# Where the inputs of the experts of rows 5 to 7 are scaled: ScalarE in four pieces, or GpSimd in two steps

## The reference, cut to what matters

```
h = h + attention(layernorm(h))
x = layernorm(h)                                   # over the 64 channels
mu, var = mean(x), var(x)
xn = (x - mu) * rsqrt(var + EPS) * gamma + beta    # 64 channels
logits = xn @ Wr + br;  w = softmax of the top 2 of 8
for e in range(8):
    hid = gelu(xn @ W1[e] + b1[e])                 # 128 wide
    y += (hid @ W2[e] + b2[e]) * w[e]
h = h + y
```

## Time and profile before

| what | value |
|---|---|
| device time, median of 3 runs | 415.62 us (415.4 to 415.87) |
| the profiled execution's own time | 415.76 us |
| its span, first to last instruction | 413.9 us |
| busy TensorE, weight loads | 389.1 us (94%), 313.9 us (76%) |
| busy VectorE, ScalarE, GpSimd | 350.8 us (85%), 324.6 us (78%), 260.3 us (63%) |
| granted TensorE clock | 1.0 over the whole span |
| the loop over the units | from about 315 us to the end |

### The profile page before, as it was taken

One profiled execution on the slowest core, in us unless ns is written; L12 is line 12 of the kernel. 1 busy time (PEld: TensorE's weight loads), 2 busy tenths in 40 slices (PEclk: granted clock), 3 DMA queues, 4 the chain that ended last, 5 costly groups with the idle time before them and its releaser, 6 DMA issues.

```text
span 413.9 us, 6363 instructions
## 1 busy us (share of the span) xinstructions
PE 389.1 (94%) x1988; PEld 313.9 (76%) x1988; DVE 350.8 (85%) x850; ACT 324.6 (78%) x555; POOL 260.3 (63%) x389
## 2 busy tenths in 40 slices
PE   5798879999999999999999998999997999998996
PEld 2586568888888888888888887877875877785773
DVE  4887689888988888898888979999987899889885
ACT  1263588999999988898887765578787999996993
POOL 0575787787778779877788466586521765343552
PEclk9999999999999999999999999999999999999999
DMA  6900010222132222212222000000000000000001
GB/s 205 357 3 0 2 25 27 53 52 47 31 51 52 34 46 52 51 34 44 52 50 52 1 1 2 1 2 1 2 2 1 1 2 13 15 13 13 14 13 26
DMA packets 15849, 14.94 MB, mean 36 GB/s; under 512 B 9796, under 2 KB 10568, under 8 KB 15560
## 3 DMA queue, kind: packets, MB, share of 16 engines
q1 hardware_dynamic: 15816, 14.54, 14.4%
HBM read 13.42 MB, written 1.11 MB: 35 GB/s over the span
## 4 chain that ended last, share of the span: by engine, by line
PE 70%; DVE 17%; ACT 5%; issue 5%; POOL 1%; DMA 1%; SPq 1%; POOLq 0%; DVEq 0%; ACTq 0%
PE ps L1497 62%; PE ps L1520 5%; DVE hid L1379 2%; ACT w_all L869 1%; DVE stats L999 1%; PE ps L1528 1%; ACT x L863 1%; DVE x L1379 1%; DVE hh L1280 1%; DVE kstat L1220 1%; DVE x L1236 1%; PE ps L1703 1%; DMA xn<-in_w_f 1%; DVE qmax L1232 1%; DVE qsum L1246 1%
## 5 line engine op out<-in xcount | busy, mean ns | idle before, releaser
L704 ACT ACTIVATE hid<-ps,b_fold 128x512 f32<-128x512 f32 x128 | 84.0, 681 | 21.3 <-PE ps L1497 20.9
L1073 DVE TENSOR_TENSOR hid_lo<-hid,hid_hi 128x1024 fp32r<-128x1024 f32 x64 | 78.7, 1229 | 25.4 <-ACT hid_hi L709 25.1
L1497 PE MATMUL ps<-xn_hi,w_all 128*128 128x512 f32 x256 | 87.4, 402 | 0.6 <-DVE xn_lo L1068 0.6
L1497 PE MATMUL ps<-hid_hi,w_all 128*128 128x512 f32 x256 | 85.0, 393 | 0.0
L709 ACT ACTIVATE hid_hi<-hid 128x1024 fp32r<-128x1024 f32 x64 | 67.9, 1061 | 2.0
L1497 PEld LDWEIGHTS ps<-xn_hi,w_all 128*128 128x128 f32 x256 | 48.4, 189 | 10.8 <-issue 0.9
L1497 PEld LDWEIGHTS ps<-hid_hi,w_all 128*128 128x128 f32 x256 | 48.1, 188 | 9.9
L1497 PE MATMUL ps<-xn_lo,w_all 128*128 128x512 f32 x128 | 49.9, 390 | 0.0
L1497 PE MATMUL ps<-hid_lo,w_all 128*128 128x512 f32 x128 | 49.8, 389 | 0.0
L1497 PE MATMUL ps<-hid_hi,ew 128*128 128x512 f32 x131 | 41.4, 402 | 0.7 <-ACT memT L807 0.4
L999 DVE BATCH_NORM_STATS2 stats<-ps 128x6 f32<-128x128 f32 x160 | 35.2, 281 | 2.8 <-PE ps L1520 2.8
(11 more groups left out here) (231 smaller groups left out, 913.0 us busy)
## 6 DMA issues: line engine op xcount, KB each, us to landing
rstd_row<-roots SPq DMA_DIRECT2D x29, 256.0 KB, 3.7
hh<-in_tokens SPq DMA_DIRECT2D x8, 256.0 KB, 7.9
hid<-in_w SPq DMA_DIRECT2D x1, 1024.0 KB, 7.2
rstd_row<-in_w SPq DMA_DIRECT2D x1, 1024.0 KB, 10.2
out<-hh SPq DMA_DIRECT2D x7, 128.0 KB, 2.0
ew_raw<-in_expert_w SPq DMA_DIRECT2D x1, 512.0 KB, 9.8
roots<-rstd SPq DMA_DIRECT2D x29, 2.0 KB, 1.4
ew_raw<-in_expert_w SPq DMA_DIRECT2D x1, 256.0 KB, 9.9
```

The source lines that it names most:

```text
L704: act.activation(hid[:, j % 2, f, :], bank[f], ACT.Gelu, bias=b1_fold[:, j // B * F + f:j // B * F + f + 1]).then_inc(gelu_done, 1)
L1073: dve.tensor_tensor(hid_lo[:, j % 2, 2 * p:2 * p + 2, :], hid[:, j % 2, 2 * p:2 * p + 2, :], hid_hi[:, j % 2, 2 * p:2 * p + 2, :].bitcast( ...
L1497: return pe.matmul(out, lhsT, rhs, start=start, stop=stop)
```

## The change

ScalarE's `ez_of` no longer runs for rows 5, 6 and 7. GpSimd does the same in a new function, `expert_input`, called right behind `expert_norm` in its order: a multiplication over all 256 columns with s spread over each tile's 64 columns, a wait for its own result, and an addition with the shift spread in the same way. Rows 0 to 4 stay as they were. ScalarE loses 12 instructions, GpSimd gets 6.

```diff
+            def expert_input(b, k):
+                pool.wait_ge(s1_ready, b + 1)
+                pool.wait_ge(ezlo_ready, b - 1)
+                v = own.inc(pool.tensor_tensor(tiles(ezf[:, k, :]), tiles(h1[:, b, :]), per_tile(s1[:, k, :], D2), ALU.mult))
+                own.wait(v)
+                pool.tensor_tensor(tiles(ezf[:, k, :]), tiles(ezf[:, k, :]), per_tile(s1_shift[:, k, :], D2),
+                                   ALU.add).then_inc(ez_ready, 1)
...
                 if n == 3:
                     expert_norm(5, 1)
+                    expert_input(5, 1)
...
                 if n == E + 3:
                     expert_norm(6, 0)
+                    expert_input(6, 0)
                 if n == 2 * E + 1:
                     expert_norm(7, 1)
+                    expert_input(7, 1)
...
-            def ez_of(b, k, tokens=range(NT)):
+            def ez_of(b, k):
...
-                if n in (7, 8):
-                    ez_of(5, 1, pair(n - 7))
...
-                if n in (2 * E - 1, 2 * E):
-                    ez_of(6, 0, pair(n - (2 * E - 1)))
...
-                if n in (2 * E + 6, 2 * E + 7):
-                    ez_of(7, 1, pair(n - (2 * E + 6)))
```

More of the change, by code:

```diff
@@ L816, in output_squares @@
                 act.activation(tiles(osq[:, k, :]), o_view(b)[:, 0, :, :], ACT.Square).then_inc(osq_ready, 1)
-            def pair(i):
-                return range(2 * i, 2 * i + 2)
-            def ez_of(b, k, tokens=range(NT)):
+            def ez_of(b, k):
                 act.wait_ge(s1_ready, b + 1)
@@ L826, in ez_of @@
                     act.wait_ge(ezlo_ready, b - 1)
-                for t in tokens:
+                for t in range(NT):
                     tile = slice(t * D2, (t + 1) * D2)
@@ L830, in ez_of @@
                                           bias=s1_shift[:, k, t:t + 1], scale=s1[:, k, t:t + 1])
-                if tokens[-1] == NT - 1:
-                    last.then_inc(ez_ready, 1)
+                last.then_inc(ez_ready, 1)
             def ez_hi(b, k):
```

## The result

The changed kernel took 418.65 us (median of 5 runs, 417.45 to 419.4), the kernel before, beside it, 415.87 us (415.4 to 417.76). The ratio is 1.0063, with a 95% interval of 1.0040 to 1.0085: slower by 1.7 to 3.5 us. I had forecast no change, 415.8 us and at most 417.2.

What follows compares the result with a forecast made beforehand. TensorE was taken as the bound, with ScalarE and VectorE nearly full too. Row 5 +0.4, row 6 0, row 7 +0.4 and the gelu stop -0.6 gave +0.2 us: 415.8 us, range 415.0 to 416.5, whole range 414.5 to 417.2.

Steps and rivals of the forecast that it cites:

- The bound: TensorE is 70% of the chain and nearly full from 346 to 362 us; ScalarE's relief can return 1.3 us at most.
- I take the longest stop, 0.6 us, as gained: TensorE's wait for the gelu of unit 30, behind row 7's removed ScalarE pairs: 0.6 us gained, bounds 0 and 1.3.
- row 5's two pairs on ScalarE: Removing them gains nothing, since TensorE's stops nearby are ended by VectorE or there are none.
- Row 5: GpSimd's added pair ahead of the split of unit 3 meets VectorE's split of unit 4: +0.4 us, bounds 0 and 0.5.
- Row 6: GpSimd's added pair ahead of the split of unit 13: 0 us, hidden by TensorE's queue, 1.54 us in hand for 1.38.
- Row 7: GpSimd's added pair makes the split of unit 17 late, onto VectorE's gate steps: +0.4 us, bounds 0 and 1.3.
- The duration of a pair: GpSimd's multiplication and addition take 0.61 us each, at most 0.83; with 0.08 us waits 1.38 us, at most 1.82.
- Behind 362 us the shift carries through: After 362 us nothing is added or removed, so the lateness there stays unchanged to the end.
- B: Rival: GpSimd's pairs and splits collide with VectorE through shared reads, 0.5 us at row 5, 1.3 at row 7; 417.4 us, chance 0.30.

Runs made afterwards that it cites:

- the two orders: Scaling of rows 5 to 7 left out on both engines, GpSimd's splits of units 9 and 23 wait for VectorE; loop 99.09 us against 99.11 in the kernel before.

## Why the prediction was wrong, point by point

- **The bound.** Right: TensorE is nearly full, and ScalarE's relief could win little. I still took 0.6 us. With the two orders set it is worth 0.02 us: ScalarE's freed time goes to waits, mostly for TensorE and VectorE.
- **The step that failed** is the term "I take the longest stop, 0.6 us, as gained", with its lower bound of 0. Its sign was wrong. The stop did go, for 0.32 us at unit 27, near the 0.33 that I had read at 353.96. But ScalarE also releases GpSimd's splits. Relieved, while VectorE was later by the other two losses, it let the split of unit 23 go ahead of VectorE's last gate step, which cost 1.00 us. I had written "0, if VectorE holds ScalarE there instead", and did not ask what an earlier ScalarE starts. The term was -0.6; from unit 26 to unit 32 the change went from 0.69 to 1.78 us late, +1.1, of which 1.00 is that step. For row 5's two pairs on ScalarE I had expected nothing; with nothing on GpSimd their going cost 0.4 us, by the split of unit 9.
- **Row 5.** Mechanism right, +0.26 instead of +0.4. The meetings came in the order that I had worked out: in times of before the multiplication ended at 323.91 and VectorE's split of unit 4 at 324.49 (323.9 and 324.5 forecast), and GpSimd's addition was held 0.36 us. It ended at 324.96 and not 325.1, and the split of unit 5 was only 0.26 us late. That nothing hides TensorE's own lateness was wrong: it was 0.77 late at unit 11 and 0.24 at unit 12, where its stop took the rest in.
- **Row 6.** Right alone: 0 forecast, 0.02 measured. TensorE's queue is not all that hid it: VectorE's split of unit 14 was held 0.85 us, which I had not foreseen, and its next meeting was shorter for it. In the whole change that lateness weighs on row 7.
- **Row 7.** Right in mechanism, and in size with row 6's share in it: 0.4 forecast, 0.44 at unit 24, of which row 7 alone makes 0.27. The rest of row 6 was shorter by 1.0 us, and the first gate step longer by as much.
- **The duration of a pair.** 0.61 and 0.61 us at row 6, 0.67 and 0.97 for the additions that met VectorE; within the bounds of 0.61 and 0.83 but for one.
- **"Behind 362 us the shift carries through".** Right to 0.02 us.
- **The rivals.** B was the nearest, 417.4 us with a loop longer by 1.8; measured 1.79. But 1.3 us were to come at row 7, from the split of unit 17 on VectorE's gate steps and its split of unit 18. Only 0.44 came there; the largest part came from the split of unit 23, through ScalarE. I looked for meetings only where GpSimd had become later, and not where it had become earlier against VectorE.
- **The range.** Its upper end of 417.2 is 415.6 + 1.6, and so short of the loop alone. The remaining 1 us of the median of 418.65 is open. The lower clock at the start explains one of the five runs; the near tie, worth 0.9 us, would fit the other three, but no run of them was profiled.

## What to carry to other kernels

Work taken off an engine makes everything that it releases earlier. Before counting the freed time as a gain, list what it releases and what then starts first at each place where two engines hold each other up. Here these places are VectorE's instructions with two operands in SBUF beside GpSimd's: a VectorE step of 0.29 us beside a GpSimd split of 1.3 us took 1.26 or 0.29 us, by which started first. Where such a pair lies on the path, a wait that lets the short one go first can be worth more than a freed engine: 1.00 us here for one wait, against 0.02 us for the relief.

## What the runs showed of the hardware

- The Trainium skill, "SBUF — State Buffer", section "Who interferes with whom", says that of the two the one that issues first holds the other up whole. The traces agree in the long steps: 1.29, 1.26, 1.34 and 1.52 us for steps of 0.21, 0.29, 0.29 and 0.42 us, and 1.00 us for the last where GpSimd had started 0.56 us ahead.
- When the two start times in a trace are 0.05 us apart, they don't tell who wins. With GpSimd's start 0.05 us ahead, VectorE's step took 1.52 us in one execution and 0.42 in another (then GpSimd's took 1.61 instead of 1.29).
- VectorE's products with one operand in PSUM were never held: all 896 in the loops of the 14 traces took 0.65 to 0.69 us, beside a split of GpSimd or not.
- The clock of TensorE was granted at 0.83 from 30 to 40 us in three of 14 executions and at 1.00 in eleven, with the same code up to there; the three began the loop 0.6 us and more after all the others.
